# A loop over pairs of batches written out as straight code, on all five engines of a mixer kernel

## What is computed

```python
def layer(x):
    xn = layernorm(x)
    logits = xn @ gate_W                              # 4 mixers, the top 2 are kept
    g, v, d = (xn @ W + b for each of 4 mixers)       # three 256x256 products for each mixer
    x_scan, a = sigmoid(g) * tanh(v), 0.001 + 0.998 * sigmoid(d)
    h = scan along the tokens: h[t] = a[t] * h[t-1] + x_scan[t]
    x = x + layernorm(sum over the chosen mixers of weight * h)
    z = layernorm(layernorm(x)) * ln_g + ln_b
    probs = softmax(batchnorm(mean of z over the tokens) @ Wr + br)      # one expert of 8 per batch
    h = relu(z @ W_down[expert] + b_down[expert])
    y = (h @ W_up[expert] + b_up[expert]) * probs[expert]
    return x + layernorm(y)
```

## Time and profile before

| what | us |
|---|---|
| median of 3 executions | 679.08 |
| lowest, highest of them | 678.12, 682.12 |
| the profiled execution | 678.97 |
| its span in the trace, first to last instruction | 677.2 |
| busy: PE (matmul), DVE, ACT, POOL | 618.5, 587.4, 461.1, 99.7 |

### The profile page before, as it was taken

One profiled execution on the slowest core, in us unless ns is written; L12 is line 12 of the kernel. 1 busy time (PEld: TensorE's weight loads), 2 busy tenths in 40 slices (PEclk: granted clock), 3 DMA queues, 4 the chain that ended last, 5 costly groups with the idle time before them and its releaser, 6 DMA issues. The chain is left out here.

```text
span 677.2 us, 10435 instructions
## 1 busy us (share of the span) xinstructions
PE 618.5 (91%) x3314; PEld 318.4 (47%) x3314; DVE 587.4 (87%) x1094; ACT 461.1 (68%) x791; POOL 99.7 (15%) x101
## 2 busy tenths in 40 slices
PE   3989999999999989999998989999998999899673
PEld 2454454445545535445544535445544554444431
DVE  6799599999899987999899987999899988889866
ACT  3728655896579675896579675896669775877404
POOL 2002011302121101302121101202030102112011
PEclk9979999999999999999999999999999999999687
DMA  8651736154712736054621737045631735211003
GB/s 224 153 187 32 156 62 237 26 111 78 253 60 54 141 101 219 1 106 93 233 80 43 144 100 228 0 96 104 209 104 43 130 99 179 44 31 32 0 22 115
DMA packets 74627, 73.27 MB, mean 108 GB/s; under 512 B 36134, under 2 KB 66122, under 8 KB 74570
## 3 DMA queue, kind: packets, MB, share of 16 engines
q1 hardware_dynamic: 69676, 56.30, 28.8%
q0 software_dynamic: 4896, 16.26, 12.9%
HBM read 38.85 MB, written 8.52 MB: 70 GB/s over the span
## 5 line engine op out<-in xcount | busy, mean ns | idle before, releaser
L1375 PE MATMUL ps_main<-xh,w_hi 128*128 128x512 f16 x768 | 292.5, 381 | 6.9 <-issue 5.7
L1375 PE MATMUL ps_main<-xh,w_lo 128*128 128x512 f16 x768 | 292.4, 381 | 0.0
L1375 PE MATMUL ps_main<-xl,w_hi 128*128 128x512 f16 x768 | 292.3, 381 | 0.0
L914 DVE TENSOR_TENSOR_SCAN hid<-decay_s,hid 128x1024 f32<-128x1024 f32 (+1 forms) x64 | 138.2, 2159 | 6.6
L581 ACT ACTIVATE hid<-ps_main,vecs 128x512 f32<-128x512 f32 x128 | 88.9, 695 | 60.5 <-PE ps_main L1375 60.1
L581 ACT ACTIVATE decay_s<-ps_main,vecs 128x512 f32<-128x512 f32 x128 | 88.9, 695 | 59.1 <-PE ps_main L1375 57.9
L1375 PEld LDWEIGHTS ps_main<-xh,w_hi 128*128 128x128 f16 x768 | 76.1, 99 | 94.6 <-issue 7.8
L581 ACT ACTIVATE gate_s<-ps_main,vecs 128x512 f32<-128x512 f32 x128 | 88.6, 692 | 44.8 <-PE ps_main L1375 43.8
L1375 PEld LDWEIGHTS ps_main<-xl,w_hi 128*128 128x128 f16 x768 | 75.4, 98 | 91.6 <-issue 1.7
L1375 PEld LDWEIGHTS ps_main<-xh,w_lo 128*128 128x128 f16 x768 | 75.3, 98 | 85.7 <-issue 1.1
L932 DVE TENSOR_TENSOR hid<-gate_s,hid 128x1024 f32<-128x1024 f32 (+1 forms) x72 | 79.5, 1105 | 6.5 <-ACT hid L581 6.0
(11 more groups left out here) (152 smaller groups left out, 606.9 us busy)
## 6 DMA issues: line engine op xcount, KB each, us to landing
comb_all<-comb_dram SPq DMA_DIRECT2D x32, 512.0 KB, 5.1
hid<-hid POOLq DMA_DIRECT2D x28, 512.0 KB, 4.6
x_in<-in_L_attn_x SPq DMA_DIRECT2D x16, 512.0 KB, 7.5
resid<-in_L_attn_x SPq DMA_DIRECT2D x8, 1024.0 KB, 6.1
out<-resid SPq DMA_DIRECT2D x7, 1024.0 KB, 5.5
expert<-experts SPq DMA_DIRECT2D x8, 192.5 KB, 2.2
hid<-hid POOLq DMA_DIRECT2D x6, 256.0 KB, 3.3
w_stage<-in_L_attn_Wg SPq DMA_DIRECT2D x4, 256.0 KB, 3.9
```

The costliest lines, as they stand in the source:

```text
L914: dve.tensor_tensor_scan(states(pc), staged(decay_s, pc, pc.c), states(pc), start, ALU.mult, ALU.add).then_inc(scanned, 1)
L1375: ins = pe.matmul(ps_main[:, i % BANKS], w[:, 3 * m + kind, k, half * P:(half + 1) * P], v[:, bt.par, span(c), k], start=(n == 0), stop=(n ...
```

## The change

The loop is replaced by a plain Python loop that emits `run` for batches 1 to 6 one behind the other. The slot numbers come out as before, and every batch number is now a plain number, so that the targets of waits and the addresses of transfers are constants. `iterations` loses its argument `eng`, in its five calls too.

```diff
-        def iterations(eng, run_first, run, last):
+        def iterations(run_first, run, last):
...
             run_first(turn(0, 0), turn(0, 1))
-            with eng.Fori(0, B // 2 - 1) as j:
-                for r in (1, 2):
-                    run(turn(j, r), turn(j, r + 1), turn(j, r - 1))
+            for n in range(1, B - 1):
+                run(turn(n // 2, n % 2), turn((n + 1) // 2, (n + 1) % 2), turn((n - 1) // 2, (n - 1) % 2))
             last(Batch(B - 1, 1, True), turn(0, B - 2))
...
-            iterations(sp, run_first, run, last)
+            iterations(run_first, run, last)
```

More of the change, by code:

```diff
@@ L526, in last @@
                 power("y", y_root_in, y_root, bt, 1)
-            iterations(pool, run_first, run, last)
+            iterations(run_first, run, last)
         @block.scalar
@@ L782, in last @@
                 scale_late_rows(bt, 1)
-            iterations(act, run_first, run, last)
+            iterations(run_first, run, last)
         @block.vector
@@ L1314, in last @@
                 finish_late(bt, 1)
-            iterations(dve, run_first, run, last)
+            iterations(run_first, run, last)
         @block.tensor
@@ L1567, in last @@
                 up(bt, 1)
-            iterations(pe, run_first, run, last)
+            iterations(run_first, run, last)
 _INS = ["L0_attn_x", "L0_attn_Wg", "L0_attn_bg", "L0_attn_Wv", "L0_attn_bv", "L0_attn_Wd", "L0_attn_bd",
```

## The result

The changed kernel takes 672.36 us in the median of 12 runs (671.75 to 675.71). The kernel before, run beside it on the same chip, takes 680.88 us (676.49 to 686.79, 12 runs). The ratio is 0.9886, 95% interval 0.9856 to 0.9915: 1.1% faster. The forecast was 672.7. The profiled execution took 672.72 us with a span of 670.6 us, 6.6 us shorter than the 677.2 before.

The account below looks back on a forecast made before the run. TensorE's matmuls were taken to set the pace, about 75.1 us per batch, with two branch gaps as pure loss. 6.05 + 0.26 = 6.31 us off 678.97 gives 672.66, plus 0.11 for the median 672.7 us; range 669.9 to 676.0.

Parts of the forecast that it names:

- Step (1): Behind batches 2 and 4: PE's two taken branches go, and their gaps with them, 2.97 + 3.08 = 6.05 us.
- rival that a hidden wait makes the gap: Behind batches 2 and 4: an untraced semaphore holds PE, only 0.17 us gained, 678.9 us; chance 0.05.
- Step (2): Behind batches 2 and 4: VectorE's branch or another engine's would not take the place of PE's gap, 0 us.
- Step (3): Register operations before waits go: 0 on PE, shorter waits before L1448 in batches 3 and 5, 0.26 us.
- Step (4): Whole straight program: fetching its code costs 0, as the loop's passes were already fetched again without gaps.
- rival of fetching: PE's queue short at gates or waits: next 16 KB code block late, about 3 us each, 681.7 us; chance 0.07.
- rival of the tail: End of the run: half-clock stretches fall otherwise on last products, 671.0 or 674.5 us; chance 0.14, half each side.
- Chances: Whole kernel, measured against 1%: 0.42 faster, 0.54 within 1%, 0.04 slower.

Follow-up runs that it names:

- e2: Changed kernel with TensorE (PE) alone keeping the three-pass loop, the other four engines straight code; 679.25 us, ratio 0.9977 to the kernel before.
- e8: The kernel before, unchanged, run and profiled again; 682.57 us, ratio 1.0028.
- e5: Kernel before with its loop kept and the backward branch announced (hint_back_edge=True); 674.8 us, ratio 0.9942.
- e1: Kernel before with TensorE (PE) alone written out straight, the other four engines looping; 676.58 us, ratio 0.9948.
- e7: Changed kernel with VectorE (DVE) alone keeping the loop, the other four engines straight code; 675.75 us, ratio 0.9931 to the kernel before.
- e3: Kernel before with one loop pass holding all six batches: register batch numbers kept, no branch taken; 673.98 us, ratio 0.9921.
- e9: Changed kernel plus eight unawaited semaphore increments on PE behind batch 2, shifting its later code; 676.25 us, ratio 0.9938 to the kernel before.
- e10: Changed kernel plus eight semaphore increments on VectorE ahead of batch 1's first statistics, shifting its code; 671.4 us, ratio 0.9844 to the kernel before.
- e11: The changed kernel, run and profiled again; 672.93 us, ratio 0.9874 to the kernel before.
- e4: Changed kernel plus a two-pass loop of one fulfilled wait on TensorE behind each of batches 1 to 6; 675.64 us, ratio 0.9919 to the kernel before.
- e6: Changed kernel plus a ten-pass loop of one fulfilled wait on TensorE behind batches 2 and 4; 682.76 us, ratio 1.0036 to the kernel before.
- e12: Repeat of e10, the changed kernel with VectorE's code eight instructions later; 671.7 us, ratio 0.985 to the kernel before.

## Why the prediction was right, and where it was not

**Step (1), PE's two taken branches, 6.05 us: right in the profiled pair.** The gaps went whole, 2.97 and 3.08 us. But the term is a property of that execution, which I took for one of the kernel. In e2 and in e8 the first gap was absent, and in e2 a gap brought low clock with it, 4.6 us. The rival that a hidden wait makes the gap is out: the gap stood where the branch took 3.5 to 3.8 us and was absent where it took 0.2 to 0.3 (e2, e5, e8).

**Step (2), VectorE's branch, 0: right in the sum, wrong in its aside.** I wrote that a stall of VectorE's would still have 0.55 us of cover if PE alone were written out. e1 and e7 show 0.7 us per branch exposed all the same, since the stall is longer than the idle time that I counted as its cover: VectorE came 0.7 us after the transposes had ended, its idle time was 1.24 us, and `down` waited 1.01. That the trace listed VectorE's branch at 62 ns had no bearing on this; the stall shows at the branch's target and not in its duration.

**Step (3), the registers, 0.26 us: too small, and only partly in place.** In the profiled pair batches 3 and 5 won 0.23 + 0.21 beyond their gaps, and batches 1 and 4 won 0.33 + 0.08, 0.85 in all. e3 puts them at 0.08 us in each of batches 3 and 4, 0.3 in batch 1, 0.6 over the six, not in two batches alone. On PE they cost nothing, as priced: with PE's alone batch 4 took 74.90 us (e2). With all but PE's it took 75.08 (e1), with VectorE's alone 75.02 (e7).

**Step (4), fetching straight code, 0: right for the net, wrong in its reason.** I read 32 packets as passes that were brought in again and again and not kept. That was so in the profiled execution, but not in all: e2 ran a pass without one packet, and e8, the same kernel, had 23. And straight code does pay: late starts of VectorE, 0.3 us in batch 2 and 0.25 in batch 6. The rival of fetching was right in kind: e9 has one exposed place in batch 5 at 78.94 - 74.99 = 3.95 us, in its longest run. Its mechanism was another, code in the way of the expert's copy; the changed kernel misses it in batches 2 to 6 by about 1 us.

The batches' account, from start to start: 3.20 + 3.29 won in batches 3 and 5, 0.33 + 0.08 in batches 1 and 4, 2 x 0.16 lost in batches 2 and 6, 6.6 in all against a forecast of 6.3. Outside them the start took 0.63 us more and the part behind batch 6 0.61 less, which cancel. So the rival of the tail, 1.7 or 1.8 us either way, didn't decide here; but it is real: from the end of batch 6 to the end of the span the profiles take 124.4 us (e10) to 128.2 (e9), and seven of the 14 have a stretch of half clock of 3.4 or 6.8 us between 572 and 586 us that the others lack. In the medians the gain is larger, 8.5 us here and 8.4 beside e11: the profiled execution of before, 678.97, lies below most of its runs. That 672.7 met 672.36 is in part luck: the forecast started 1.8 us below the median of 12 runs and left out 2.2 us of the gain. Half clock behind a gap, as in e2, would account for the long runs. No trace of a run above 680 of the kernel before was taken, but the mean granted clock is on record for 83 other runs of it (e8 among them): 0.974 in the 28 of 678 to 680 us, 0.969 in the 23 above 683, which makes 35 and 42 us at the lower level. Where TensorE sets the pace, 7 us more at half speed cost an estimated 3.4 of the 5.3 us between the two groups. Where in the run they stood is not shown. Chances: the forecast lay 0.9% down, just short of the 1% bound, and the result 1.1%.

The Trainium skill's page "Runtime: NRT & Kernel Launch", section "Instruction fetch mechanics", says that a branch that leaves the window it describes must wait for a fetch. The stalls of 3.5 to 3.8 us agree. The same section gives the instruction memory as 128 KiB for TensorE and 32 KiB for most engines, and in a note as only two lines of 16 KiB. With 26 packets of 16 KB for eight batches on q8 after the change, a body of two batches is an estimated 6.5 packets, 107 KB. By the note's two lines every taken branch back over it would stall, and e2's first, 239 ns with no packet from 230 to 390 us, did not; the 128 KiB would hold it. But e2's second branch, over the same body in the same execution, took 3756 ns and brought nine packets. So the size alone doesn't decide, and what does stays open.

## What to carry to other kernels

Look for idle time labelled "issue" on the engine that sets the pace and lay it beside the branch's own duration in the trace. Take more than one profile: the same branch took 0.24 us in one pass and 3.5 in the next. Here such stalls were worth 1.1%, and a loop with its backward branch announced gave more than half of it without longer code. Write out all engines together or look for the next stall: with PE alone straight, VectorE's branch gave back 0.7 us per pass.

A difference of 1 to 3 us between two versions of such a kernel may be no more than where code blocks end. Shift the code by a few idle instructions before you believe it, and compare the time behind the changed stretch too.

## What the runs showed of the hardware

- A taken branch of TensorE over a body of two batches took 226 to 253 ns in some cases and 3526 to 3756 ns in others, and both within one execution of the kernel before (239 and 3541 ns, e8).
- With a 16 KB code packet starting 1.2 or 2.2 us behind the issue of a copy of 192.5 KB, nine of the copy's 144 packets came late: 3.8 us (e4, e6) and 4.6 us (e9) to landing instead of 2.2. With the code packet 0.1 to 0.8 us behind the issue it was 2.7 to 3.2 us.
- VectorE started an instruction at three places, 63 over a multiple of 128 in its count, up to 0.36 us late with nothing else to hold it, the same three in both profiles of the changed kernel. With eight more instructions ahead none was late (e10, e12).
- Behind idle stretches of TensorE of 2.4 to 3.1 us the granted clock fell to the 1.2 GHz level for about 3 us in e2, e6 and e9, and stayed at 1.00 behind the 2.81 us of the earlier trace rows and behind e6's first gap of 2.57 us. The length of the idle time alone doesn't tell which.
